# Attention pooling for a recommender: unread products put into TensorE's pauses during the first two chunks

## What is computed

```python
W_b, W_c = (fc1_w[:E], fc1_w[E:])
h = jax.nn.relu(jnp.einsum('bse,eh->bsh', behavior_emb, W_b) + (candidate_emb @ W_c)[:, None, :] + fc1_b)
scores = jnp.einsum('bsh,h->bs', h, fc2_w[:, 0]) + fc2_b[0]
attn = jax.nn.softmax(scores, axis=-1)
user_interest = jnp.einsum('bse,bs->be', behavior_emb, attn)
x = jnp.concatenate([user_interest, candidate_emb], axis=1)
z = jax.nn.relu(x @ mlp1_w + mlp1_b)
logit = (z @ mlp2_w + mlp2_b)[:, 0]
```

## Time and profile before

| | us |
|---|---|
| median of 3 runs | 278.26 |
| lowest and highest run | 276.95, 279.87 |
| the profiled execution, its own time | 279.17 |
| its span, first to last instruction | 277.4 |
| TensorE busy with matmuls | 266.2 |
| VectorE busy | 233.5 |
| ScalarE busy | 215.4 |
| mean granted TensorE clock | 0.988 |

### The profile page before, as it was taken

The page is one execution under the profiler, slowest core; times in us unless marked ns, Lnnn a source line. Parts: engine busy times, 40 slices in busy tenths (PEclk is TensorE's granted clock), DMA queues, the critical chain, the costliest instruction groups (busy, mean ns, idle before and its releaser), DMA issues.

```text
span 277.4 us, 8724 instructions
## 1 busy us (share of the span) xinstructions
PE 266.2 (96%) x2998; PEld 200.2 (72%) x2998; DVE 233.5 (84%) x405; ACT 215.4 (78%) x557; POOL 28.8 (10%) x38
## 2 busy tenths in 40 slices
PE   5969999999999999999999999999999999999895
PEld 4645678777777777887777777787777777777663
DVE  1809999999999999999999999999999999999451
ACT  3466788888889988888888898888888889888412
POOL 2000111111011111111100111111110011111100
PEclk9995999999999999999999999999999999999999
DMA  7999999999999999999999999999999999992000
GB/s 234 438 426 419 433 421 423 423 426 423 428 426 425 432 421 430 425 426 426 430 425 426 430 421 430 425 426 426 430 425 426 430 423 432 421 430 97 0 2 1
DMA packets 10506, 105.84 MB, mean 382 GB/s; under 512 B 1152, under 2 KB 1664, under 8 KB 2432
## 3 DMA queue, kind: packets, MB, share of 16 engines
q1 hardware_dynamic: 10352, 105.39, 90.2%
q10 hardware_dynamic: 144, 0.31, 0.3%
HBM read 105.70 MB, written 0.00 MB: 381 GB/s over the span
## 4 chain that ended last, share of the span: by engine, by line
PE 92%; DVE 2%; ACT 2%; DMA 2%; issue 1%
PE z_ps L577 19%; PE s_ps L594 17%; PE z_ps L581 17%; PE z_ps L578 17%; PE u_ps L604 16%; DMA first_sb<-in_first 2%; PE z_ps L604 1%; DVE xl L440 1%; PE u_ps L701 1%; ACT hidden L355 1%; PE u_ps L632 1%; DVE hidden L450 1%; PE z_ps L673 1%; PE z_ps L667 1%; ACT xh L311 1%
## 5 line engine op out<-in xcount | busy, mean ns | idle before, releaser
L440 DVE TENSOR_TENSOR xl<-xt,xh 128x800 fp32r<-128x800 f32 x128 | 123.9, 988 | 9.4 <-ACT xh L311 8.9
L311 ACT CAST xh<-xt 128x800 fp32r<-128x800 f32 x128 | 108.5, 880 | 1.0 <-DMA xt<-in_behavior_t 0.8
L577 PE MATMUL z_ps<-xh,w_hi 128*128 128x512 f32 (+1 forms) x256 | 95.9, 375 | 3.1 <-ACT xh L311 2.2
L355 ACT ACTIVATE hidden<-z_ps,bias 128x200 f32<-128x200 f32 x256 | 89.2, 442 | 11.7 <-PE z_ps L581 10.5
L578 PE MATMUL z_ps<-xh,w_lo 128*128 128x512 f32 (+1 forms) x256 | 86.7, 353 | 0.0
L450 DVE TENSOR_TENSOR hidden<-z_ps,neg_bias 128x800 f32<-128x800 f32 x64 | 63.2, 988 | 8.7 <-PE z_ps L581 8.3
L581 PE MATMUL z_ps<-xl,w_hi 128*128 128x512 f32 (+1 forms) x256 | 69.6, 354 | 0.0
L577 PEld LDWEIGHTS z_ps<-xh,w_hi 128*128 128x128 f32 x256 | 49.5, 193 | 20.4 <-ACT xh L311 7.4
L604 PEld LDWEIGHTS u_ps<-x,weights_by_row 128*32 128x32 f32 x1500 | 46.5, 110 | 12.3 <-issue 12.3
L578 PEld LDWEIGHTS z_ps<-xh,w_lo 128*128 128x128 f32 x256 | 50.0, 195 | 6.2 <-issue 0.3
L594 PE MATMUL s_ps<-hidden,f_col 128*1 128x384 f32 (+1 forms) x512 | 50.1, 509 | 1.4 <-issue 1.4
(11 more groups left out here) (69 smaller groups left out, 83.8 us busy)
## 6 DMA issues: line engine op xcount, KB each, us to landing
x<-in_behavior SPq DMA_DIRECT2D x32, 1600.0 KB, 17.5
xt<-in_behavior_t SPq DMA_DIRECT2D x31, 1600.0 KB, 15.6
xt<-in_behavior_t SPq DMA_DIRECT2D x4, 400.0 KB, 5.5
first_sb<-in_first ACTq DMA_DIRECT2D x1, 307.5 KB, 4.9
later_sb<-in_later SPq DMA_DIRECT2D x1, 258.5 KB, 22.5
cand<-in_candidate SPq DMA_DIRECT2D x1, 192.0 KB, 5.4
cand<-in_candidate SPq DMA_DIRECT2D x1, 64.0 KB, 4.6
out_logit<-logit SPq DMA_DIRECT2D x1, 1.8 KB
```

What stands on the lines that cost most here:

```text
L311: nc.scalar.copy(xh[g][:, :], xt[q][:, g, :]).then_inc(xh_made, 1)
L355: op = nc.scalar.activation(hidden[q % 2][:, g, :, mine], z[:, :, mine], ACT.Relu, bias=bias[:, bass.ds(c * ROWS + g * EACH + b, 1)])
L440: nc.vector.tensor_tensor(xl[g][:, :], xt[q][:, g, :], xh[g][:, :].bitcast(F32), ALU.subtract).then_inc(xl_made, 1)
L577: nc.tensor.matmul(z[:, a:b], w_hi[:, :], xh[g][:, a:b], start=True, stop=False)
```

## The change

`keep_busy(bank, n)` is new. It issues n products of `ones` with `ones`, 128x128 by 128 columns, into the first 128 columns of a PSUM bank. It has no wait and signals nobody, and nothing reads what it writes: each of the banks is overwritten by a later product, or its earlier content has been copied. `WARM_UP` goes from 7 to 10.

```diff
-WARM_UP = 7
+WARM_UP = 10
...
+            def keep_busy(bank, n):
+
+                for _ in range(n):
+                    nc.tensor.matmul(bank[:, 0:P], ones[:, :], ones[:, :], start=True, stop=True)
+
             pe.wait_ge(ones_made, 1)
             for n in range(WARM_UP):
                 op = nc.tensor.matmul(z_ps[0][:, 0:P], ones[:, :], ones[:, :], start=True, stop=True)
             op.then_inc(warm, 1)
             pe.wait_ge(first_loaded, 16)
             transpose_candidates(0)
+            keep_busy(u_ps, 2)
             bias_products(0)
+            keep_busy(s_ps, 2)
             pe.wait_ge(w_lo_made, 1)
 
             def period(c, q, phase):
@@ -715,8 +722,13 @@
                     if phase == 0 and g == 0:
                         transpose_candidates(1)
                         bias_products(1)
+                        keep_busy(s_ps, 4)
                     if phase == 0 and g == 2:
                         shift_sums()
+                    if phase == 0 and g == GROUPS - 1:
+                        keep_busy(s_ps, 10)
+                    if phase == 1 and g == 0:
+                        keep_busy(s_ps, 3)
                     if g == PHASE_AT and phase >= 1:
                         score(c - 1, (q + 1) % 2, phase == 1)
```

## The result

The changed kernel takes 277.06 us (median of 20 runs, 276.60 to 277.39), the kernel before 278.87 (20 runs, 276.95 to 280.28). The ratio is 0.9938, interval 0.9924 to 0.9951: 1.8 us faster, which is under the 1% of the prediction's bound. The range, 276.9 to 281.1, held the time, the sign was wrong: +0.7 us was forecast. The scatter of single runs went from 3.3 us to 0.8.

A forecast was written before the change was run, and what follows sets the result against it. TensorE, busy 96% of the span, was taken as the bound, with VectorE pacing 20 to 39 us. A fall's 1.4 less the rise's 0.7 gave +0.7 us on the 278.26 median: 279.0, range 276.9 to 281.1.

The forecast's parts named there:

- a new fall: TensorE's pause before 31.0 us grows from 0.36 to 2.1 us, so the clock drops again: 1.4 us lost.
- an early rise: Chunk 0: clock up before group 0 ends; 2.45 us gained, 1.75 paid for six products, so 0.7 us gained.
- I put the rise at about 9.8: Start of chunk 0: high clock from about 9.8 us, between 5.3 and 16.6, with the pause at 6.4 to 7.03 filled.
- the three products of the warm-up: Start of the kernel: 1.3 us more, hidden while TensorE waits until 5.96 for the candidates; effect nothing.
- The gain case's floor: Rise right behind the warm-up, no fall: candidates' part and group 0 also run high, a further 1.0 us, 276.5.
- a rival: Early rise and no fall in the later pause: 277.6 us, down to 276.5 with the earliest rise; chance 25%.
- The restored clock in 20.0 to 26.8 itself buys nothing: Chunk 1: VectorE has no idle time there, so its maximum releases TensorE at the same time whatever TensorE's clock.
- the four products on the path at the high clock: Ahead of group 1 of chunk 0, which stood ready: 0.9 us at the high clock, 1.7 at the low.
- the three and the first two that are covered: Behind group 0 of chunk 1, 0.65 us covered at the high clock; behind the first transpose, nothing or 0.1.
- the ten that end just in time: Behind group 3 of chunk 0: 2.2 us at the high clock into a 2.22 us pause, ending at 20.0.
- no load bounds the middle of the run: Whole run: ScalarE waited for a load once, 0.8 us, so a start-up moved by one or two us meets none.
- The two ahead of group 0: Behind `bias_products(0)` in chunk 0, no pause filled: 0.85 us at the low clock on the path.

The follow-up runs named there:

- e8_long_pause: e3_no_six with one more unread VectorE maximum ahead of the one that releases TensorE, lengthening TensorE's pause there; 278.36 us.
- e7_warm7_no_six: e3_no_six with a warm-up of 7 products in place of 10; 276.95 us.
- e2_fills_only: The changed kernel with the old warm-up of 7 and all other fills kept; 278.12 us.
- e1_warm_only: The kernel before with the warm-up of 10 products alone, none of the other fills; 276.80 us.
- e3_no_six: The changed kernel without the two products before group 0 and the four before group 1 of chunk 0; 276.03 us.
- e11_copy_first: e3_no_six with ScalarE's copy of the other candidates moved ahead of the high half of group 2; 276.72 us.
- e4_no_late: The changed kernel without the ten products behind group 3 of chunk 0 and the three behind group 0 of chunk 1; 277.84 us.
- e9_long_pause_filled: e8_long_pause with ten unread products behind group 0 of chunk 2 filling the lengthened pause; 276.60 us.

## Why the prediction was wrong

The forecast was a sum, 1.4 us for a new fall less 0.7 for an early rise. The fall did not come, and the rise gave 1.8. That the range held 277.06 is luck in part: it began at 276.9, 1.4 us under the 278.26 that three runs had given for the kernel before, and 20 runs gave 278.87, so a gain of 1.8 us lay outside what the range meant.

**The rise of the clock was put too late.** "I put the rise at about 9.8" was the middle of a span from 5.3 to 16.6. The record of the changed kernel starts at 5.81, those of the other kernels with 10 products at 3.83 to 6.04, but for e8_long_pause (10.42). What I priced at nothing, the three products of the warm-up, is what moves it in most executions: with 7 it is 9.4 and 9.8 (e7_warm7_no_six, e2_fills_only), and the three without any other fill give 276.80 us (e1_warm_only). For the rise at 9.81 the sum holds, 0.9 us measured for 0.7. The gain case's floor had the other end, 0.7 + 1.0 = 1.7 us, and 1.8 was measured. So the size of the gain was in the text, under a rival.

**The fall was forecast from a pause that was worked out too long.** The mechanism is shown: at 2.53 us the clock falls in ten of twelve executions and costs 1.8 us, for which I had 1.4. But the pause in the changed kernel is 1.63 us and not 2.1, and it leaves the clock alone (a mean clock of 0.998 or more in all 20 runs). The start of chunk 1's group 1 was right to 0.05 us against VectorE's start (2.94 us behind it, I had 2.9). From there I added 1.1, 1.5 and 3 x 1.1 = 5.9 from start to start. TensorE's last row ends at 27.54, which is 6.3 us behind 21.24: about 0.15 is the pipeline's end, which the 0.36 of before had already left out, and 0.25 are transitions that I left out (group 1 takes 1.27 from its start to the scores, group 2 1.20 to the next). And the release came 10.87 us behind VectorE's start where I had 11.0. Three small terms make 0.5 us, on a step where half a microsecond decides. The bounds that I had, a fall 1.5 us into a pause and none at 1.38, did not say what a pause between them and 2.2 us does, and I took them as saying "over 1.5". By the runs 1.63 to 1.65 us did no harm in the 26 of the changed kernel and e3_no_six, 1.77 was followed by a fall in four of ten executions (e11_copy_first) and 2.2 in all eleven of e4_no_late, so with the pause as I had put it, 2.1, the fall might well have come. That was not run.

**"The restored clock in 20.0 to 26.8 itself buys nothing" was wrong too**, by 0.5 to 0.8 us (e4_no_late). It was all but true of the kernel before, where the scores and VectorE were tied; I read "no idle time" off VectorE's timeline, and the chain's rows over TensorE, 23.63 to 27.92, said that any later scores would be paid for. Once chunk 1 starts 2 us earlier and the clock stays low as long, the scores at 2.90 us are late for VectorE.

**Right were** the four products on the path at the high clock (0.9 forecast, 0.8 measured), the three and the first two that are covered, the ten that end just in time, and that no load bounds the middle of the run. The two ahead of group 0 were priced at 0.85 and cost some 0.2: at the high clock they are half, and a load covers them. That load, which became the first link of the chain, was no step of the prediction. The wait for `bias_f2` grew to 0.99 us (1.1 forecast).

**The rule of the Trainium skill** (TensorE: Matmul & The Clock Gate, "Why this matters for your kernels"), which warns only of longer pauses, came out right for this kernel and not for the kernel before or for the variants: e8_long_pause falls 2.4 us into a pause, e4_no_late 0.95 us into one of 2.2 us, e11_copy_first behind one of 1.77 us, and e1_warm_only behind two of under 1 us. Where they differ the rows decide.

What stays open is why a pause of 1.63 us is harmless in all 20 runs of the changed kernel while the clock fell 1.5 us into the pause of the kernel before. That pause went on to 2.2 us; how the moment of the fall is set was not tried. Open too is why the rise came at 10.42 in one profile with ten products in the warm-up.

## What to carry to other kernels

Unread products pay where they bring the clock up before the first work and where they cover a pause of about 2 us or more (0.8 us for the thirteen late ones here, 1.8 for the ten of e9_long_pause_filled). Where real work stands ready behind them they are only cost: taking out the six here gave 1.0 us beyond the change, 276.03 us in all; no kernel timed was below that. Time each group of them alone: here the three of the warm-up give the whole gain by themselves, the thirteen late ones give 0.8 us and the six take 1.0. Read the chain in full before calling an engine free: VectorE had no idle time, and still the next late instruction would have been TensorE's. Before trusting a threshold, measure both sides as the profile measures them, from the modelled end of one row to the start of the next, and give the threshold case a chance and not the forecast when the margin is half a microsecond. A wide scatter of a kernel's runs can itself be the clock's doing at its start: with three products more in the warm-up and none of the others, six of seven runs lay within 0.9 us, where the kernel before has 3.3.

## What I had not expected of the hardware

The clock's rise is not tied to the kernel's own time: with the same warm-up of 10 it came at 3.83, 3.98, 4.00, 4.12, 4.39, 4.48, 4.82, 5.81, 6.04 and 10.42 us in single profiles. The scores at the low clock took 2.90 us against 1.55 at the high (1.98 in the mixed case of the earlier trace rows), a price of 1.35 us, more than the 0.9 of a whole group. And a fall need not come at a pause's end or at a fixed distance into it: it came 0.95, 1.5 and 2.4 us into pauses of 2.2 to 2.5 us, and, behind the end of one, 1.3 us in e1_warm_only (at 21.46) and 0.4 us in e11_copy_first. Nor does the same pause always bring it: of the same kernel, ten of twelve executions fell (e8_long_pause), or four of ten (e11_copy_first).
